# Roots for pairs of tiles on ScalarE and VectorE, one normalising operation, and projections ahead of turns, in a four-level transformer

## The reference, cut to what matters

```
def _layernorm(x, axis=-1, eps=1e-05):
    m = jnp.mean(x, axis=axis, keepdims=True)
    v = jnp.var(x, axis=axis, keepdims=True)
    return (x - m) / jnp.sqrt(v + eps)
...
h = tok(x)                               # patches @ W + b + pos_emb
h = h + L0_attn(_layernorm(h))           # delays, one head of 192, softmax
h = h + L0_ffn(_layernorm(h))            # 8 linear experts, top 2, softmax
h = h + L1_attn(_layernorm(h))           # 12 heads, q, k, v, scores, context quantised; + bproj
h = h + L1_ffn(_layernorm(h))            # four T5 layers, two with 8 experts, a last norm (eps 1e-6)
h = h + L2_attn(_layernorm(h))           # 12 heads, rope, causal softmax; + bo
h = h + L2_ffn(_layernorm(h))            # 16 experts, top 2, adds its input
h = h + L3_attn(_layernorm(h))           # 12 heads, partial rope, softmax; + bo
h = h + L3_ffn(_layernorm(h))            # 16 experts, top 8
```

## Time and profile before

| | us |
|---|---|
| median of 3 runs (1633.18, 1648.29, 4505.66) | 1648.29 |
| profiled execution | 1638.03 |
| its span | 1636.3 |
| TensorE busy | 1381.3 (84%) |
| VectorE busy | 591.0 (36%) |
| ScalarE busy | 508.8 (31%) |
| GpSimd busy | 574.1 (35%) |
| granted TensorE clock, mean | 0.904 of full speed |

### The profile page before, as it was taken

One profiled execution on the slowest core, in us unless ns is written; L12 is line 12 of the kernel. 1 busy time (PEld: TensorE's weight loads), 2 busy tenths in 40 slices (PEclk: granted clock), 3 DMA queues, 4 the chain that ended last, 5 costly groups with the idle time before them and its releaser, 6 DMA issues. The chain is left out here.

```text
span 1636.3 us, 35722 instructions
## 1 busy us (share of the span) xinstructions
PE 1381.3 (84%) x14530; PEld 1046.4 (64%) x14530; DVE 591.0 (36%) x1577; ACT 508.8 (31%) x1387; POOL 574.1 (35%) x848
## 2 busy tenths in 40 slices
PE   6669657999998996899999899668569996995997
PEld 4354325888876895688877688624458884362756
DVE  2436562333334212333343411235431112443434
ACT  3330434343441111334343111234313334432120
POOL 2031654222322564323232256454326564350000
PEclk8769858999999998899999899879669998977999
DMA  3100202000003531200000353200044442100000
GB/s 128 39 10 5 97 1 88 3 2 2 12 15 142 176 124 62 90 2 2 2 15 12 150 190 102 91 26 5 27 184 137 165 159 77 37 3 29 30 29 19
DMA packets 40625, 101.96 MB, mean 62 GB/s; under 512 B 15952, under 2 KB 26324, under 8 KB 35344
## 3 DMA queue, kind: packets, MB, share of 16 engines
q0 software_dynamic: 18480, 58.56, 10.4%
q1 hardware_dynamic: 20256, 38.77, 7.0%
q10 hardware_dynamic: 1728, 2.36, 0.5%
HBM read 138.21 MB, written 11.50 MB: 91 GB/s over the span
## 5 line engine op out<-in xcount | busy, mean ns | idle before, releaser
L1396 PE MATMUL bank<-t_ew,t_hg 128*128 128x192 f32 x552 | 97.2, 327 | 0.0
L1433 ACT ACTIVATE t_hg<-bank 128x384 f32<-128x384 f32 x92 | 40.1, 488 | 178.0 <-PE bank L1384 110.1
L2300 POOL TENSOR_SCALAR t_rstd<-t_ssq 128x1 f32<-128x1 f32 x64 | 12.3, 192 | 219.9 <-ACT t_junk L2136 219.7
L1396 PEld LDWEIGHTS bank<-t_ew,t_hg 128*128 128x128 f32 x552 | 88.7, 190 | 0.2
L1708 DVE SCALAR_TENSOR_TENSOR h<-bank,cw,h 128x192 f32<-128x192 f32 x128 | 53.5, 418 | 87.4 <-PE bank L1631 70.3
L1429 ACT ACTIVATE l_hg<-bank,l_ew 128x128 f32<-128x128 f32 x186 | 51.4, 375 | 105.7 <-PE bank L1384 61.5
L1380 PE MATMUL bank<-t_xgT,t_ew 128*128 128x128 f32 x552 | 71.3, 279 | 13.0 <-DVE t_xgT L1474 11.6
L1282 POOL DMA_INDIRECT t_ew<-in_t_moe,source x46 | 47.5, 1033 | 91.0 <-DVE t_og L1483 45.7
L1380 PEld LDWEIGHTS bank<-t_xgT,t_ew 128*128 128x128 f32 x552 | 67.4, 193 | 16.8 <-DVE t_xgT L1474 14.3
L210 PE MATMUL bank<-blk,ident 128*128 128x384 f32 x96 | 49.3, 628 | 32.7 <-issue 19.7
L2057 PE MATMUL bank<-t_wo,t_ctx 128*128 128x192 f32 x384 | 71.0, 335 | 0.9 <-ACT t_ctx L2153 0.9
(11 more groups left out here) (367 smaller groups left out, 3115.2 us busy)
## 6 DMA issues: line engine op xcount, KB each, us to landing
t_qkv<-in_t_wqkv SPq DMA_DIRECT2D x9, 576.0 KB
t_wo<-in_t_wo SPq DMA_DIRECT2D x8, 576.0 KB
w<-in_l_w SPq DMA_DIRECT2D x8, 576.0 KB, 4.1
wA<-in_t_wqkv SPq DMA_DIRECT2D x2, 1728.0 KB
patches<-in_patches SPq DMA_DIRECT2D x8, 384.0 KB, 5.7
rows_in<-rows SPq DMA_DIRECT2D x24, 128.0 KB, 1.7
t_wi<-in_t_wi SPq DMA_DIRECT2D x3, 576.0 KB
t_gg<-rows_out ACTq DMA_DIRECT2D x8, 192.0 KB, 4.4
```

The costliest lines, as they stand in the source:

```text
L1396: mm = pe.matmul(k.bank[6 + b % 2][:, 0:DIM], k.hg[b % 2][:, m, :], w[:, SPLIT + m * DIM:SPLIT + (m + 1) * DIM], start=(m == 0), stop=(m = ...
```

## The change

Tiles fall in five groups, (0,1), (2,3), (4,5), (6) and (7), and the root is formed once for a group. `deviations` takes the square root on ScalarE, and `norm_behind` the reciprocal and the offset on VectorE, in the embedding, out projection, linear experts, quantised attention, final normalisation and the tail of the level 2 experts. In the embedding and the out projection VectorE normalises as well. In the two compact attentions, where ScalarE runs exponentials, the root stays on GpSimd, for a group at a time. `normalise` is one instruction of 192 columns (one more of 64 where the rows are also stored), and `turn_tile` makes the second copy of channels 128 to 191 by a matmul with the identity, three TensorE instructions instead of two. The number of banks for turned tiles rises from two or one to four, or to a list of eight. In the compact attention the projections of tiles 6 and 7 go ahead of the turns and logits, and in the last four tiles all turns ahead of all logits. The bias of the quantised attention is added to `h` by GpSimd in the linear experts' phase instead of by VectorE in the quantised projection, and the quantised attention adds the projection ahead of the context's evacuation.

```diff
+    k.eps = sb("eps", [P, 1])
...
-            for t in range(NT):
-                root(k, pool, t)
...
-            for s in range(NT + 1):
-                if s < NT:
-                    normalise(k, act, k.h, s, k.xn[:, s, :])
-                t = s - 1
+            act.wait_ge(k.quant_a, 1)
+            for s in range(NT + 4):
+                deviations(k, act, s)
+                t = s - 4
                 if t >= 0:
...
+            dve.memset(k.eps[:], 1e-5).then_inc(k.quant_a, 1)
...
-            step = stats_behind(k, dve, k.h, k.added)
+            step = norm_behind(k, dve, k.h, k.added, here=True)
...
+GROUPS = ((0, 2), (2, 4), (4, 6), (6, 7), (7, 8))
+GROUP_OF = [next(g for g, (a, b) in enumerate(GROUPS) if a <= t < b) for t in range(NT)]
+def group_ending(t):
+    return next((g for g, (_, b) in enumerate(GROUPS) if b == t + 1), None)
+def norm_behind(k, dve, src, done, here=False):
+    def step(t):
+        if t < NT:
+            dve.wait_ge(done, t + 1)
+            dve.bn_stats(k.stats[:, t, :], src[:, t, :]).then_inc(k.seen, 1)
+        g = group_ending(t - 1)
+        if g is not None:
+            tiles = slice(*GROUPS[g])
+            dve.wait_ge(k.root_step, g + 1)
+            dve.reciprocal(k.rstd[:, tiles], k.std[:, tiles]).then_inc(k.inverted, 1)
+        if t < NT:
+            dve.wait_ge(k.seen, t + 1)
+            dve.bn_aggr(k.mv[:, t, :], k.stats[:, t, :]).then_inc(k.measured, 1)
+        if g is not None:
+            dve.wait_ge(k.inverted, g + 1)
...
+            if here:
+                for n in range(*GROUPS[g]):
+                    dve.tensor_scalar(k.xn[:, n, :], src[:, n, :], k.mv[:, n, 0:1], k.rstd[:, n:n + 1], ALU.subtract,
+                                      ALU.mult).then_inc(k.tile_normed, 1)
+            else:
+                dve.scalar_tensor_tensor(k.offset[:, tiles], k.mv[:, tiles, 0], -1.0, k.rstd[:, tiles], ALU.mult,
+                                         ALU.mult).then_inc(k.rooted, 1)
+    return step
+def deviations(k, act, t):
+    g = group_ending(t)
+    if g is not None:
+        tiles = slice(*GROUPS[g])
+        act.wait_ge(k.measured, t + 1)
+        act.activation(k.std[:, tiles], k.mv[:, tiles, 1], ACT.Sqrt, bias=k.eps[:, 0:1]).then_inc(k.root_step, 1)
...
+    g = group_ending(t)
+    if g is None:
+        return
+    tiles = slice(*GROUPS[g])
+    inv = k.rstd[:, tiles]
     pool.wait_ge(k.measured, t + 1)
-    pool.tensor_scalar(inv, k.mv[:, t, 1:2], 1.0, eps, ALU.mult, ALU.add).then_inc(k.root_step, 1)
-    pool.wait_ge(k.root_step, 2 * t + 1)
-    pool.tensor_tensor(inv, inv, k.power[:, 0:1], ALU.pow).then_inc(k.root_step, 1)
-    pool.wait_ge(k.root_step, 2 * t + 2)
-    pool.tensor_scalar(k.offset[:, t:t + 1], k.mv[:, t, 0:1], inv, -1.0, ALU.mult, ALU.mult).then_inc(k.rooted, 1)
-def normalise(k, act, src, t, dst=None):
-    act.wait_ge(k.rooted, t + 1)
-    if dst is not None:
-        parts = [(dst, src[:, t, :])]
-    else:
-        parts = [(k.rows[:, t, 0:P], src[:, t, 0:P]),
-                 (k.rows[:, t, P:ROW].rearrange("p (c f) -> p c f", c=2),
-                  src[:, t, P:DIM].unsqueeze(1).broadcast_to([P, 2, REST]))]
-    for to, x in parts:
-        ins = act.activation(to, x, ACT.Identity, bias=k.offset[:, t:t + 1], scale=k.rstd[:, t:t + 1])
+    pool.tensor_scalar(inv, k.mv[:, tiles, 1], 1.0, eps, ALU.mult, ALU.add).then_inc(k.root_step, 1)
+    pool.wait_ge(k.root_step, 2 * g + 1)
+    pool.tensor_tensor(inv, inv, k.power[:, tiles], ALU.pow).then_inc(k.root_step, 1)
+    pool.wait_ge(k.root_step, 2 * g + 2)
+    for n in range(*GROUPS[g]):
+        ins = pool.tensor_scalar(k.offset[:, n:n + 1], k.mv[:, n, 0:1], k.rstd[:, n:n + 1], -1.0, ALU.mult, ALU.mult)
+    ins.then_inc(k.rooted, 1)
+def normalise(k, act, src, t, dst, doubled=False):
+    act.wait_ge(k.rooted, GROUP_OF[t] + 1)
+    scales = dict(bias=k.offset[:, t:t + 1], scale=k.rstd[:, t:t + 1])
+    ins = act.activation(dst, src[:, t, :], ACT.Identity, **scales)
+    if doubled:
+        ins = act.activation(k.rows[:, t, DIM:ROW], src[:, t, P:DIM], ACT.Identity, **scales)
     ins.then_inc(k.tile_normed, 1)
...
-def turn_tile(k, pe, t, banks):
+def turn_tile(k, pe, t, banks, ring=0):
     pe.wait_ge(k.tile_normed, t + 1)
-    if t >= len(banks):
-        pe.wait_ge(k.tile_kept, t + 1 - len(banks))
+    ring = ring or len(banks)
+    if t >= ring:
+        pe.wait_ge(k.tile_kept, t + 1 - ring)
     bank = k.bank[banks[t % len(banks)]]
-    pe.transpose(bank[:, 0:P], k.rows[:, t, 0:P], k.ident[:])
-    pe.transpose(bank[:, P:2 * P], k.rows[:, t, P:ROW], k.ident[:]).then_inc(k.tile_turned, 1)
+    pe.transpose(bank[:, 0:P], k.xn[:, t, 0:P], k.ident[:])
+    pe.transpose(bank[0:REST, P:2 * P], k.xn[:, t, P:DIM], k.ident[:])
+    pe.matmul(bank[REST:P, P:2 * P], k.xn[:, t, P:DIM], k.ident[:], start=True, stop=True).then_inc(k.tile_turned, 1)
...
-            pool.wait_ge(k.std_in, 1)
-            pool.tensor_tensor(k.std[:], k.var[:], k.power[:], ALU.pow).then_inc(k.std_out, 1)
-            for s in range(NT + 3):
-                t = s
-                if t < NT:
-                    pool.wait_ge(k.normed, t + 1)
-                    pool.tensor_tensor(k.h[:, t, :], k.h[:, t, :], k.xn[:, t, :], ALU.add).then_inc(k.added, 1)
-                t = s - 3
-                if t >= 0:
-                    root(k, pool, t)
+            for t in range(NT):
+                pool.wait_ge(k.normed, t + 1)
+                pool.tensor_tensor(k.h[:, t, :], k.h[:, t, :], k.xn[:, t, :], ALU.add).then_inc(k.added, 1)
...
             link(dve.tensor_tensor(k.var[:], mean, mean, ALU.mult))
             link(dve.tensor_tensor(k.var[:], k.var[:], var, ALU.add))
             dve.tensor_scalar(k.var[:], k.var[:], eps, None, ALU.add).then_inc(k.std_in, 1)
             dve.wait_ge(k.std_out, 1)
-            for t in range(NT + 3):
+            link(dve.reciprocal(k.var[:], k.var[:]))
...
         def _(act):
-            for s in range(NT + 1):
-                if s < NT:
-                    normalise(k, act, k.h, s)
-                if s >= 1:
-                    keep_tile(k, act, s - 1, (6, 7))
+            act.wait_ge(k.std_in, 1)
+            act.activation(k.var[:], k.var[:], ACT.Sqrt).then_inc(k.std_out, 1)
+            for s in range(NT + 3):
+                if 0 <= s - 2 < NT:
+                    normalise(k, act, k.h, s - 2, k.xn[:, s - 2, :])
+                if s >= 3:
+                    keep_tile(k, act, s - 3, (4, 5, 6, 7))
+                deviations(k, act, s)
...
+                turn_tile(k, pe, t, (4, 5, 6, 7))
...
-                    turn_tile(k, pe, i - 5, (2, 3))
...
+                deviations(k, act, i - 2)
...
+            step = norm_behind(k, dve, dst, k.evacuated_v, here=True)
...
+    turn_banks = (7, 7, 7, 7, 0, 1, 2, 3)
...
+            def output(t):
+                pe.wait_ge(k.ctx_copied, t + 1)
+                if t >= 1:
+                    pe.wait_ge(k.added, t)
+                parts = project(t)
+                for i, (lhsT, w) in enumerate(parts):
+                    mm = pe.matmul(p_bank, lhsT, w, start=(i == 0), stop=(i == len(parts) - 1))
+                mm.then_inc(k.projected, 1)
+            def logits(t):
+                if t == 0:
+                    pe.wait_ge(k.loaded, 16 * len(loads))
+                tile_logits(k, pe, t, n_e)
+            def turn(t):
+                turn_tile(k, pe, t, turn_banks, ring=1 if t < 4 else NT)
+            for s in range(NT + 2):
                 t = s
                 if t < NT:
                     if t >= 2:
                         pe.wait_ge(k.biased, t - 1)
                     idle_products(pe, k, s_bank(t), 1)
                     score(pe, t, s_bank(t)).then_inc(k.scores, 1)
-                t = s - 4
-                if 0 <= t < NT:
...
+                if 4 <= s:
+                    output(s - 4)
...
-                    tile_logits(k, pe, t, n_e)
-                t = s - 8
-                if 0 <= t < NT:
-                    turn_tile(k, pe, t, (7,))
+                if s == NT + 1:
+                    for t in range(NT - 2, NT):
+                        output(t)
+                if s >= 8:
+                    logits(s - 8)
+                if s >= 7:
+                    turn(s - 7)
+            logits(2)
+            turn(3)
+            logits(3)
+            for t in range(4, NT):
+                turn(t)
+            for t in range(4, NT):
+                logits(t)
...
-                    step(t)
-            step(NT)
-            step(NT + 1)
+                    dve.wait_ge(k.added, t + 1)
+                    dve.bn_stats(k.stats[:, t, :], dst[:, t, :]).then_inc(k.seen, 1)
+                    dve.wait_ge(k.seen, t + 1)
+                    dve.bn_aggr(k.mv[:, t, :], k.stats[:, t, :]).then_inc(k.measured, 1)
...
-                if s >= 6:
-                    root(k, pool, s - 6)
+                if s >= 4:
+                    root(k, pool, s - 4)
...
```

(68 more changed lines are left out.)

92 lines of the change are left out of this document (31 added, 61 removed).

## The result

The changed kernel takes 1637.6 us (median of 20 runs), the kernel before 1644.2 us on the same chips. The ratio is 0.9961, 95% interval 0.9943 to 0.998: 6.4 us faster, with 3 to 9 in the interval. A second comparison, on chip 1, where the kernel before takes 1628.4 us, gave 0.9947 (0.9918 to 0.9976). I had forecast 21 us, and 1617 us in a range from 1600 to 1635; the median lies just outside it.

A forecast was written before the change was run, and what follows sets the result against it. TensorE was taken to bound the level 2 attention tail, small operations of VectorE, ScalarE and GpSimd the quantised attention. Terms 1.7 + 2.8 + 2.3 + 0.6 + 10 + 2.7 + 1.3 = 21.4 off 1638.0 gave 1616.6; range 1600 to 1635.

The forecast's parts named there:

- The quantised attention, -10: Largest term: two ScalarE stalls behind GpSimd offsets go, phase ends near 243.0 instead of 253.1; -10 us (8 to 11.5).
- The 2.3 us lost to the reordered addition: Quantised attention's tail: adding the projection ahead of the context's evacuation was to cost 2.3 us.
- rival 4: Six added ScalarE table loads are exposed, costing 7.7 us; 1624 us in all; chance 0.07.
- Level 2 and level 3 attention, 0 each: Compact attentions: level 2's stretch after the last value product takes 18.0 us at 1.10 a turn; 0 each (+1.5 to -7).
- the final normalisation: Shorter root at the chain's head, first turn 2.8 us earlier, TensorE's pace before and after; -2.7 us (1 to 4).
- level 2 expert tail, -1.3: Last two tiles leave through GpSimd's queue of roots; saving one queue turn gives -1.3 us (0 to 3).
- the out projection: Roots leave GpSimd, only copies stay on ScalarE, TensorE sets the pace; -2.8 us (1.9 to 4.5).
- Rival 2: Only the quantised attention pays; three-operation turns make TensorE-bound tails give back the root's gain; 1625 us, chance 0.20.
- Rival 1: Attention tails: denser TensorE work keeps the clock at 2.4 GHz, -7 us each, 1603 us; chance 0.18.
- Rival 3: Quantised attention: stalls move to VectorE waiting for the projection, -10 becomes -3, 1624 us; chance 0.07.
- rival 5: Loops with root steps: ScalarE and VectorE stall on each other in order, 4.4 us a time, 1670 us; chance 0.03.
- The low end of the gain (11 us): Whole kernel: sum of all terms' low bounds, 11 us less, about 1625 us.

The follow-up runs named there:

- the quantised attention's kernels: Kernel before with only the quantised attention changed: 0.9947; with only its normalisation moved behind the tile's work: 0.9947; with the changed phase but root and normalisation ahead: 0.9934.

## Why the prediction was wrong, step by step

**What held.** The quantised attention, -10, came at -10.8 and -10.9, by the mechanism in the trace: the two steps of 8 us went. That its size fits is in part luck. The 2.3 us lost to the reordered addition are not there, so other terms of that sum gave less than I took; and the step did grow to about 4 us, but not by the addition. A root from the Sqrt to the offset takes 0.68 us for the 0.7 worked out. The linear experts (-2.0, -2.9 for -2.3) are within their bounds. The embedding (-2.9, -1.8 for -1.7) gained more than its bound of 2.5 once, and the quantised projection (-0.5, +0.5 for -0.6) lost once. The table loads, costed at nothing, show 0.6 us in the final normalisation, 0.6 in the out projection and 0.3 in the expert tail: 1.5 at most, not the 7.7 of rival 4.

**The step that failed** is the price of the turn, in "Level 2 and level 3 attention, 0 each". I took 1.10 us for it from the embedding, from the first start to the last modelled end, as a turn of the same form. It is not: the embedding's turn is one transpose and the product, and the new turn has a second transpose, of half width (L431 above). It takes 1.24 us from start to start. The old turn I had at 0.54, and it takes 0.43 to 0.49. So a turn costs about 0.77 us more, not 0.56. TensorE's timeline of the level 2 attention, after:

```profile
1157.30 0.34 PE L888 MATMUL bank<-l_ptb,l_vx 32*32 32x32 f32 x11 [0.26 <-issue]
...
1163.87 0.61 PE L450 MATMUL bank<-wr,xT 128*128 128x16 f32 x2 [0.47 <-ACT xT L439]
...
1166.73 0.61 PE L450 MATMUL bank<-wr,xT 128*128 128x16 f32 x2 [0.47 <-ACT xT L439]
...
1176.53 0.61 PE L451 MATMUL bank<-wr,xT 64*128 64x16 f32 x2
```

The last value product ends at 1157.6 and the phase's last product at 1177.1: 19.5 us for the 18.0 that I worked out, and 17.3 before. Six turns at 0.14 are 0.8 of the difference. The rest is the wait of 0.47 for the copy, twice, which I had struck out: it still stands before the logits of the first tiles, whose turns share one bank. (The projections behind the value product are two and not three, and with a wait of 0.54 between them they take 3.6 us for 3.8.) The remaining 1.4 us of the loss lie ahead of that point (36.2 us into the phase for 34.8), where two of the eight turns and one pair of logits stand in the loop, for one turn before; I had priced none of this. Level 2 came out at +3.6 and +4.4. Level 3 came at -2.2 and +0.7; in five profiles of kernels that leave it as it was it takes 49.8 to 54.5 us, so that is not told from 0.

**The same price was left out of three other terms.** For the final normalisation I wrote that the pace before and after is TensorE's, and then did not add the turn's cost to it. At the higher clock the first half of that was wrong as well, by the idle 0.19 us above. The first turn did come earlier, at 1073.35 for 1075.12 before, 1.8 us of the 2.8. But the pace went from 1.27 to 1.42 us a tile at the higher clock and from 1.83 to 2.62 at the lower, and the phase gained 0 and 0.7 us for 2.7. With two transposes it gained 3.1. In the level 2 expert tail, -1.3, the stretch from the first statistics to the end takes 17.4 and 17.1 us for 17.0 before, and 15.0 with two transposes; the phase's own rows hide this, since the experts ahead of it differ by more from chip to chip. In the out projection, -0.8 and -3.0 for -2.8, one of two profiles holds the forecast. The runs show what the omission weighs: three operations alone cost the old kernel 23 us, and taking them out of the changed one gives 11 by the ratios and 9 by the phases named here and level 2.

**Rival 2** ("only the quantised attention pays", 1625, chance 0.20) named the mechanism that decided: three operations a turn cost more, and each tail bound by TensorE gives back what the root gains. It had about the right total, -13, for what the rows of the table show, -12 and -10. I gave it less than half the chance of the forecast although the row of 5.88 of 6.00 us speaks for it. Rival 1 did not come in level 2, where the granted clock in the tail is 0.50. In level 3 it is 0.73 and 0.62 in the two profiles, for 0.50 and 0.55 before, without the 7 us; the quantised attention's kernels have up to 0.79 there with the old phase, so it is not the denser work that did it. Rival 3 did not come, rival 4 in a fifth of its size, and the stalls of rival 5 are there in kind but not on the path. VectorE's timeline in the final normalisation has one, with TensorE busy through it:

```profile
1080.18 0.17 DVE L365 RECIPROCAL rstd<-std 128x2 f32<-128x2 f32 x1 [3.04 <-ACT std L389]
```

**What the range missed besides.** The low end of the gain (11 us) let no term for TensorE be a loss of more than 1.5 us. The profiled execution from which I summed was 6 us below the median that 20 runs gave, and I did not allow for it; -6.4 from 1644.2 gives 1637.6, while the table's -10 to -12 from 1638 would have given 1627, inside the range. Of the 21 us between 1616.6 and 1637.6, some 6 are this base, 9 are the phases, and 6 are open: the timed difference falls short of the phases' sum by that in the first pair, more than its interval allows, and by 1 in the second. And the sign that I had set, a phase that the change does not touch moving by more than 2 us, tells nothing: the T5 layers of the old kernel did so by 14 between two profiles.

## What to carry to other kernels

An edit that takes instructions off one engine and puts them on another is to be priced at the second engine's start-to-start time, in every phase in which that engine is full, also where the phase is cited for something else. Where an engine waits in order on a small result of another, look at what stands behind the wait: moving the waiting instruction behind the work that is ready gave 7 us here, without a single instruction saved. And before two profiles are compared by their total, cut them at their barriers, take both from one chip, and look at the granted clock of each stretch before a difference is put down to an edit.

## What the runs showed of the hardware

The four T5 layers, with the same instructions, took 798.9 to 826.1 us in fourteen profiles. The two stretches of experts in them took 123 to 127 us on chip 1 and 128 to 132 elsewhere, and the clock does not account for that: in the kernel before the first stretch has 128.3 us at a granted clock of 0.96, with 119 GB/s moved, in one profile, and 123.4 at 0.93, with 124 GB/s, in the other. A float32 product with the identity of 128x64 by 128x128 is shown as two instructions. At the lower clock it takes TensorE 0.62 us to the next start, the transpose of the same block ahead of it 0.35, and one of a full block 0.21 to 0.27. The Sqrt on 128x2 with a bias took 0.29 us, not the 0.21 of the 128x8 row that I had taken for it. A table load behind a barrier ran while ScalarE waited for its data, but for 0.6 us in one case; in the middle of a loop it held up the Sqrt and the copy behind it, and in the embedding it began only when the data of its Sqrt was there.
